# A cross-attention and FFN layer on one core: new instruction sequences on all engines, with some sums and small steps moved

## The reference

```python
sim = (ctx @ Wq.T per head) . (ctx @ Wk.T per head), summed over 4 heads, scaled      # 512 x 512 per batch
threshold = the 153rd largest of each row of sim
A = sigmoid(sim) * (sim >= threshold);  A = (A + A.T) * 0.5
g = sigmoid(gamma_raw)
x = x + (1 - g) * layernorm(x) + g * A
z = layernorm(x)
# bitlinear(v, w): v is RMS-normed and rounded to 8 bits per row, w is rounded to -1, 0, 1 by its mean |w|
x = x + bitlinear(silu(bitlinear(z, w_gate)) * bitlinear(z, w_up), w_down)
```

## Time and profile before

| what | us |
|---|---|
| median of 3 runs (lowest, highest) | 289.45 (288.89, 290.41) |
| the profiled execution's own time | 291.13 |
| its span, first to last instruction | 289.3 |
| first gate matmul to the last final | 75.3 to 286.9 |
| busy: TensorE, VectorE, ScalarE, GpSimd | 212.6, 226.1, 191.9, 191.7 |

### The profile page before, as it was taken

The page is one execution under the profiler, slowest core; times in us unless marked ns, Lnnn a source line. Parts: engine busy times, 40 slices in busy tenths (PEclk is TensorE's granted clock), DMA queues, the critical chain, the costliest instruction groups (busy, mean ns, idle before and its releaser), DMA issues.

```text
span 289.3 us, 3730 instructions
## 1 busy us (share of the span) xinstructions
PE 212.6 (73%) x916; PEld 99.6 (34%) x926; DVE 226.1 (78%) x355; ACT 191.9 (66%) x352; POOL 191.7 (66%) x380
## 2 busy tenths in 40 slices
PE   7760001322888876979995997798979999999874
PEld 6320001320333333434342543333344444444332
DVE  0388784998979999899859889989879994959621
ACT  2697799899979979976475899732427643731500
POOL 2156778877897966788878867787754774507330
PEclk9996555575599999999998899999979999999999
DMA  5999999937840794331321643205030534180592
GB/s 134 381 387 365 365 210 377 278 134 219 162 95 19 121 184 82 74 68 36 61 71 22 178 76 72 56 0 128 3 72 0 106 96 91 27 192 13 110 243 109
DMA packets 78970, 39.21 MB, mean 136 GB/s; under 512 B 67936, under 2 KB 70240, under 8 KB 78432
## 3 DMA queue, kind: packets, MB, share of 16 engines
q1 hardware_dynamic: 78944, 38.94, 53.7%
HBM read 17.96 MB, written 4.19 MB: 77 GB/s over the span
## 4 chain that ended last, share of the span: by engine, by line
PE 24%; POOLq 23%; issue 17%; POOL 17%; ACT 8%; DVE 7%; DVEq 2%; ACTq 0%
PE DN L380 8%; PE U L366 8%; PE G L352 7%; POOLq L809 4%; POOLq L839 3%; POOL S L899 3%; POOLq L811 3%; POOL X L835 2%; POOL X L842 2%; ACT S L513 2%; POOLq L799 2%; ACT WuT L506 2%; ACT junk_c L464 2%; POOL srch L812 2%; POOL sig L783 2%
## 5 line engine op out<-in xcount | busy, mean ns | idle before, releaser
L489 ACT ACTIVATE sg<-G,gsc 128x1024 f32<-128x1024 f32 x32 | 35.5, 1110 | 48.7 <-PE G L352 38.3
L366 PE MATMUL U<-WuT,xqT 128*128 128x512 bf16 x256 | 63.5, 393 | 5.3 <-DVE S L670 5.3
L352 PE MATMUL G<-WgT,xqT 128*128 128x512 bf16 x256 | 62.2, 387 | 3.8 <-ACT sg L489 3.8
L380 PE MATMUL DN<-WdT,S 128*128 128x512 bf16 x246 | 56.7, 380 | 8.7 <-DVE X L696 8.2
L670 DVE TENSOR_TENSOR S<-U,sg 128x1024 f32<-128x1024 f32 x32 | 39.0, 1219 | 12.8 <-PE U L366 9.0
L899 POOL TENSOR_SCALAR S<-S,qh 128x2048 int16<-128x2048 f32 x16 | 31.8, 1990 | 25.6 <-DVE qh L686 24.9
L464 ACT ACTIVATE junk_c<-rows,srch 128x512 int8<-128x512 f32 x64 | 45.3, 711 | 5.1 <-POOL srch L812 4.3
L380 PEld LDWEIGHTS DN<-WdT,S 128*128 128x128 bf16 x256 | 24.8, 98 | 40.8 <-issue 12.9
L366 PEld LDWEIGHTS U<-WuT,xqT 128*128 128x128 bf16 x256 | 25.1, 101 | 39.2 <-DVE S L670 9.9
L352 PEld LDWEIGHTS G<-WgT,xqT 128*128 128x128 bf16 x256 | 25.1, 100 | 36.6 <-issue 5.5
L675 DVE TENSOR_REDUCE amh<-S 128x1 f32<-128x2048 f32 x16 | 36.4, 2274 | 0.1
(11 more groups left out here) (127 smaller groups left out, 382.3 us busy)
## 6 DMA issues: line engine op xcount, KB each, us to landing
S<-in_L_ffn_w_gate SPq DMA_DIRECT2D x4, 1024.0 KB, 10.3
X<-in_x SPq DMA_DIRECT2D x4, 1024.0 KB, 7.0
S<-in_L_ffn_w_up SPq DMA_DIRECT2D x4, 1024.0 KB, 13.8
S<-in_L_ffn_w_down SPq DMA_DIRECT2D x4, 1024.0 KB, 9.3
out<-X SPq DMA_DIRECT2D x16, 256.0 KB, 2.6
C<-in_ctx SPq DMA_DIRECT2D x2, 256.0 KB, 5.8
C<-in_ctx SPq DMA_DIRECT2D x1, 512.0 KB, 13.9
xqT<-qx SPq DMA_TRANSPOSE x16, 2.5
```

The source lines that it names most:

```text
L352: last = nc.tensor.matmul(G[:, c * 512:(c + 1) * 512], xqT[:, t, k, :], WgT[:, 4 * n:4 * n + 4, k, :], start=(k == 0), stop=(k == KD - 1))
L366: last = nc.tensor.matmul(U[:, c * 512:(c + 1) * 512], xqT[:, t, k, :], WuT[:, 4 * n:4 * n + 4, k, :], start=(k == 0), stop=(k == KD - 1))
L380: last = nc.tensor.matmul(DN[:, :], hqT[:, i % 2, k, :], WdT[:, k, :], start=(k == 0), stop=(k == KF - 1))
L489: A(sg[:, u % 2, :], G[:, :], ACT.Silu, scale=gsc[:, b % 2, t:t + 1]).then_inc(silu_done, 1)
```

## The change

All five lists are in another order. Beside that: the sums of the search (mean and variance of half a row of sim) come from VectorE's `bn_stats` and `bn_aggr` (`sim_stats`) and no longer from ScalarE, and the first threshold is three GpSimd instructions instead of eight; all four sums of w_down are on ScalarE (three were on VectorE); `x_scale`, `x_round` and `x_cast` of the first batch go tile by tile; the reciprocal of hfl moved from GpSimd (a power of -1) to VectorE (`h_floor`); `ln_coef` has fewer steps; for the last tile the absolute maximum, the rounding (now on VectorE), the cast and the transpose go by halves; and the last four downs write four different banks, so that they no longer wait for each other's `final`.

```diff
+        def down_bank(i):
+
+            return (DN, AT, SIM, TR)[i % NT] if i >= TILES - NT else DN
 
...
-        ABS_ACT = ((1,), (0, 1, 2, 3), (3,))
+        ABS_ACT = ((1,), (0, 1, 2, 3), (0, 1, 2, 3))
...
+            def hT_last(hs):
+                i = TILES - 1
+                sp.wait_ge(hq_last, hs + 1)
+                sp.wait_ge(down_psum, i - 1)
+                sp.dma_start_transpose(hqT[:, i % 2, hs * KF // 2:(hs + 1) * KF // 2, :],
+                                       hq[:, i % 2, hs * HF:(hs + 1) * HF]).then_inc(hqT_last[hs], 16)
+
...
-            w_load(0, w_gate, 0); w_load(0, w_gate, 1); c_load(0, 1, 2); x_load(0); w_load(0, w_gate, 2)
...
+            x_load(0); c_load(0, 1, 2); w_load(0, w_gate, 0); w_load(0, w_gate, 1); w_load(0, w_gate, 2)
+            w_load(0, w_gate, 3); w_load(1, w_up, 0); c_load(1, 2, 4); x_load(1); w_load(1, w_up, 1); x_load(2)
+            w_load(1, w_up, 2); w_load(1, w_up, 3); w_load(2, w_down, 0); w_load(2, w_down, 1); w_transpose(0, 0)
...
+                if i == TILES - 1:
+                    pe.wait_ge(hqT_last[hs], 16)
+                elif hs == 0:
+                    pe.wait_ge(hqT_ready[i % 2], 16 * (i // 2 + 1))
                 if hs == 0:
-                    pe.wait_ge(hqT_ready[i % 2], 16 * (i // 2 + 1))
...
+                    elif i <= TILES - NT:
+                        pe.wait_ge(final_done, i)
                     else:
-                        pe.wait_ge(final_done, i)
+                        pe.wait_ge(x1_ready, NT * B)
                 for k in range(hs * KF // 2, (hs + 1) * KF // 2):
-                    last = nc.tensor.matmul(DN[:, :], hqT[:, i % 2, k, :], WdT[:, k, :],
+                    last = nc.tensor.matmul(down_bank(i)[:, :], hqT[:, i % 2, k, :], WdT[:, k, :],
...
-                    if a:
-                        act.wait_ge(thr_act, 2 * ROUNDS * (a - 1) + j // 2 + 1)
-                    A(ROWS[a % 2][:, j, :], sim_bank(a, j), ACT.Copy, accum_out=sum1[:, j:j + 1]).then_inc(sim_ready, 1)
-
-            def sim_sq(a, j):
-
-                act.wait_ge(sim_ready, NT * a + j + 1)
-                if NT * a + j >= 2:
-                    act.wait_ge(simstat, NT * a + j - 1)
-                A(junk_s[:, j % 2, :], ROWS[a % 2][:, j, 0:N // 2], ACT.Square, accum_out=sum2[:, j:j + 1]).then_inc(simstat, 1)
+                    A(ROWS[a % 2][:, j, :], sim_bank(a, j), ACT.Copy).then_inc(sim_ready, 1)
...
+            def sim_stats(a, *js):
+
+                for j in js:
+                    dve.wait_ge(sim_ready, NT * a + j + 1)
+                    V.bn_stats(bns[:, j, :], ROWS[a % 2][:, j, 0:N // 2])
+                dve.drain()
+                for j in js:
+                    last = V.bn_aggr(mvs[:, j, :], bns[:, j, :])
+                last.then_inc(simstat, 1)
 
...
+            def x_scale(a, *js):
+
+                c = slice(js[0], js[-1] + 1)
+                dve.drain()
+                V.tensor_scalar(amf[:, c], amx[:, c], D * Q_EPS * (LN_EPS * RMS_EPS) ** 0.5, 1.0 / 127.0,
+                                ALU.max, ALU.mult)
+                dve.drain()
+                V.reciprocal(qsx[:, c], amf[:, c]).then_inc(qsx_ready, len(js))
...
+            def last_absmax(hs):
+
+                i = TILES - 1
+                dve.wait_ge(mul_done, 2 * i + hs + 1)
+                V.tensor_reduce(amh[:, i % 4:i % 4 + 1] if hs == 0 else aml[:, 0:1],
+                                h[:, i % 2, hs * HF:(hs + 1) * HF], AX.X, ALU.max, apply_absolute_value=True)
+
+            def last_scale():
+                i, c = TILES - 1, slice((TILES - 1) % 4, (TILES - 1) % 4 + 1)
+                dve.wait_ge(hcoef, i - 3)
+                dve.drain()
+                V.scalar_tensor_tensor(amh[:, c], amh[:, c], aml[:, 0:1], hfl[:, (B - 1) % 2, NT - 1:NT],
+                                       ALU.max, ALU.max)
+                dve.drain()
+                V.tensor_scalar(amc[:, c], amh[:, c], 1.0 / 127.0, None, ALU.mult)
+                dve.drain()
+                V.reciprocal(qh[:, c], amc[:, c]).then_inc(qh_ready, 1)
+
+            def last_round(hs):
+                i, f = TILES - 1, slice(hs * HF, (hs + 1) * HF)
+                dve.drain()
+                if hs == 0:
+                    dve.wait_ge(hqT_ready[i % 2], 16 * (i // 2))
+                V.tensor_scalar(hq[:, i % 2, f].bitcast(I16), h[:, i % 2, f], qh[:, i % 4:i % 4 + 1], 1.0,
+                                ALU.mult, ALU.mult)
+                dve.drain()
+                V.tensor_copy(hq[:, i % 2, f], hq[:, i % 2, f].bitcast(I16)).then_inc(hq_last, 1)
+
+            def h_floor(a):
+
+                dve.wait_ge(xcoef, a + 1)
+                V.reciprocal(hfl[:, a % 2, :], hfl[:, a % 2, :])
+
...
-                pool.wait_ge(simstat, NT * a + 2 * p + 2)
-                G_.tensor_scalar(sims_m[:, js], sum1[:, js], 1.0 / N, 0.0, ALU.mult, ALU.add)
-                G_.tensor_scalar(sd[:, js], sum2[:, js], 2.0 / N, 0.0, ALU.mult, ALU.add)
-                pool.drain()
-                G_.tensor_tensor(ptmp[:, js], sims_m[:, js], sims_m[:, js], ALU.mult)
-                pool.drain()
-                G_.tensor_tensor(sd[:, js], sd[:, js], ptmp[:, js], ALU.subtract)
-                pool.drain()
-                G_.tensor_scalar(sd[:, js], sd[:, js], 0.0, 1.0, ALU.max, ALU.mult)
-                pool.drain()
-                G_.tensor_tensor(sd[:, js], sd[:, js], bc(root, 2), ALU.pow)
+                pool.wait_ge(simstat, 2 * a + p + 1)
+                G_.tensor_tensor(sd[:, js], mvs[:, js, 1], bc(root, 2), ALU.pow)
                 pool.drain()
                 G_.tensor_scalar(ptmp[:, js], sd[:, js], -START_Z, 0.0, ALU.mult, ALU.add)
                 pool.drain()
-                G_.tensor_tensor(nthr[:, js], ptmp[:, js], sims_m[:, js], ALU.subtract).then_inc(thr_act, 1)
+                G_.tensor_tensor(nthr[:, js], ptmp[:, js], mvs[:, js, 0], ALU.subtract).then_inc(thr_act, 1)
 
...
-                G_.tensor_tensor(su2[:, a % 2, :], usc[:, a % 2, :], usc[:, a % 2, :], ALU.mult)
-                pool.drain()
-                G_.tensor_tensor(hfl[:, a % 2, :], hfl[:, a % 2, :], bc(inv, NT), ALU.pow).then_inc(xcoef, 1)
-
```

243 lines of the change are left out of this document (121 added, 122 removed).

## The result

The changed kernel takes 285.15 us in the median (284.09 to 286.1, 4 runs), the kernel before beside it 289.17 (288.72 to 290.41): a ratio of 0.985, 95% interval 0.9811 to 0.9888. The profiled execution took 285.98 us with a span of 284.2, against 291.13 and 289.3. The prediction was 288.4, so the kernel became faster, and by more than forecast: 4.0 us between the medians and 5.1 us between the profiled spans, where the sum said 1.05.

The account below looks back on a forecast made before the run. VectorE was taken to set T, the last batch's first transpose, with fixed TensorE work and the tail behind it. From 289.45: -2.3 + 3.45 + 3.45 - 5.65 = -1.05 gave 288.4 us; range 283.5 to 294, forecast's own 286 to 290.8.

Parts of the forecast that it names:

- Start (-0.5): Head up to about 91 us: new load order and moved sums put VectorE 0.5 us ahead.
- Rival 3: Start of the FFN late: first gate at 76.5, second at 88; 291.4 us if 3 us get through; chance 0.07.
- T: Moment of TensorE's first transpose of A of the last batch, 211.37 us before; forecast to move -2.3, to about 209.
- VectorE's added work up to T (+4.0): VectorE before the last batch's transposes: search sums, reciprocals and `mul(19)` added, `final(6)` removed; +4.0 us.
- The waits (-3.3): VectorE's waits from 91.5 to 211.3 us, 5.3 us without the branch, shrink by 3.3 us.
- The stretching (-2.5): VectorE's mask products and quantizations running longer than needed, 5.0 us in all; half goes, -2.5 us.
- Rival 1: VectorE hung on GpSimd; all its waits and stretching go, T moves -6.8, time 283.9 us; chance 0.22.
- The sign of being wrong in kind: TensorE reaching the last batch's transposes after the mask was ready would mean TensorE bounds the middle; no size given.
- Rival 2: Slower: added sums fall on VectorE, the full engine, and nothing comes back; T +3.5, time 294.2 us; chance 0.20.
- Rival 4: Collisions of VectorE with GpSimd stay, waits shrink: the stretching's 2.5 us don't come, 290.9 us; chance 0.08.
- Behind T (+6.9): TensorE after the last batch's first transpose: `down(7)` and `down(12)` now run there, +3.45 us each.
- Tail (-5.65): From the last up's end to the program's end: 15.1 us in place of 20.75, -5.65 us.

Follow-up runs that it names:

- run 3: Changed kernel with the last batch's four mask products one behind the other after `mul(19)`; 0.993 of the kernel before.
- run 2: Changed kernel with five small GpSimd instructions added ahead of each first threshold, search sums still on VectorE; 1.010 of the kernel before.
- Run 9: Kernel before with only the search sums moved to VectorE and the first threshold cut to three GpSimd instructions; 1.019 of the kernel before.
- Run 4: Changed kernel with three of w_down's four sums back on VectorE; 0.999 of the kernel before.
- run 12: Changed kernel with four list moves against waits, then `mul(16)` and others moved earlier too; 0.987 of the kernel before.
- Runs 5 and 6: Changed kernel with one bank for all downs, 0.995 of the kernel before; changed kernel with the last tile whole again, 1.000.
- Runs 1: Changed kernel with the search sums back on ScalarE and the first threshold again in eight GpSimd instructions; 1.017 of the kernel before.

## Why the prediction was right or wrong

*Start (-0.5).* First weight sum at 12.87 (said 12.4), first gate at 76.46 (76.5), second gate at 90.83 (said 88). But VectorE is not ahead at 91 us. A row of before, then one of after:

```profile
90.36 1.22 DVE L670 TENSOR_TENSOR S<-U,sg 128x1024 f32<-128x1024 f32 x1
```

```profile
92.03 1.21 DVE L688 TENSOR_TENSOR S<-U,sg 128x1024 f32<-128x1024 f32 x1
```

The first is `mul(1)`, the second `mul(0)`. So at 91.0 the changed kernel lacks two `mul`, 2.4 us, that the kernel before had done at 91.5, and is one mask product (0.7) ahead: +1.2 and not -0.5. Rival 3's lateness was there; by T it was more than made good.

*VectorE's added work up to T (+4.0).* Sized about right. By count and mean of the lines the sums added 3.5 us (a pair 0.75 + 0.25 as said, 414 ns for a `bn_stats` of 256 elements), the floors 0.5 and `mul(19)` 1.2, and 0.5 of `final(6)` went behind T: +4.7. With the two `mul` and the mask product of the start it is 6.4 us more in the stretch. Against it stands an item that the prediction didn't have: where one VectorE instruction follows another without a pause, their rows overlap by some 0.08 us, and the durations less the busy time are 1.6 us more after than before.

*The waits (-3.3).* The size came out, in part by luck. VectorE's time without an instruction is 119.8 - 106.03 = 13.8 us before and 116.0 - 105.82 = 10.2 after, -3.6. The waits alone (eight groups before, not seven) fell by as much, 9.2 to 5.6; the short pauses stayed. Of the 5.3 us that I had bounded 3.6 are left, -1.7 and not -3.3. The other 2.0 are the gap between two `pick` products, which I had taken for the branch's and left out. It lay beside GpSimd's products, so it probably belongs to the same collisions as the stretching; that is argued from the rows, and no run moved it alone.

*The stretching (-2.5).* This is the term that was most off. It gave -4.9: the mask products -3.6 (all of my bound), the quantizations -1.0, `rank`'s product +1.7, and the small products over eight elements 8 x (430 - 224) = -1.6, with 0.4 in smaller ones; I had seen none of these last as stretched. I took half where all came, since I tied the stretching to GpSimd's big tiles, which stay. What counts is which instruction stands beside them: run 3 shows that the order of four calls is worth 753 against 997 ns.

In all: the stretch begins 0.5 earlier, and 6.4 of work, -4.9 of stretching, -1.6 of overlap and -3.6 of waits give -4.2, where T moved by -4.4; the rest is rounding. Against the forecast's -2.3 the start was 1.7 us worse and the work 0.7, the stretching 2.4 better, the waits 0.3 better, and the overlap, 1.6, was not in the sum.

*Rival 1 (GpSimd was what VectorE hung on).* Its price of -6.8 at T was not reached, but run 2 speaks for its mechanism: forty small GpSimd instructions cost 7 us of the total, and in the head they stand ahead of a sum that VectorE waits for. Run 9 limits it: in the old lists the relief, together with the sums on VectorE, gives nothing.

*The sign of being wrong in kind.* I had written that TensorE reaching the transposes after the mask was ready would mean that TensorE bounds the middle. It did, by 0.15 us. Run 4 says that the reading would be false: VectorE work added in the head, while ScalarE had less, moved T by 4.4 us, and again no wait is seen there. TensorE's own arrival hangs on VectorE's products ahead of it, here `mul(16)`, and in run 12, where that comes early, TensorE waits for VectorE at three later places. The sign was badly chosen.

*Rival 2 (added sums on the full engine).* It did not come in the new lists, and it is what run 9 shows in the old ones: 1.019. The points that the prediction gives for it are wrong by its own sum: with -0.5 + 4.0 at T, 6.9 behind and -5.65 in the tail the time moves by 4.75 less what VectorE saves, so the zero lies at 4.75 us of the 10.3 and not at 1.0, and a loss that can be told (1.45 us) at 3.3 and not at 2.5. The forecast of 5.8 saved was 1.05 from no change at all.

*Rival 4 and the rule on SBUF.* The Trainium skill (SBUF — State Buffer, "Who interferes with whom") says that a VectorE instruction with two SBUF inputs contends with a GpSimd instruction that reads SBUF. For an instruction with one input the same section of the Trainium skill rules this out only outside the 2-port modes, which `cast` and `tensor_scalar` can enter, and the prediction left that exception out. This case agrees on the first: the mask products, `rank`'s product and the `pick` products have two inputs, while the reductions of 2048 columns stayed at 2277 ns. The stretched ones with a single input are of the kinds of the exception: the quantizations (1159 and 810 ns in the mean, where the median of all eight is 690), and in run 12 a cast and one of the two instructions on four columns; the other has two inputs. GpSimd's big instructions ran beside all three of run 12 (rows above). No run shows whether these were in such a mode. And I drew the wrong thing from the rule, that the collisions would stay because the big instructions do.

*Behind T (+6.9).* Measured +5.2. The two downs are 3.45 each, but I took what stood behind T as fixed, and 1.7 us of it were TensorE's slow clock after its wait before: the up at 212.51 had taken 3.37 us at a granted clock of 0.56, with the stretch's clock at 0.97, now 1.89 and 1.00. In this execution the wait cost twice, and I counted it once. It doesn't always: in run 9 the same wait of 2.23 us was followed by a clock of 1.00 and an up of 1.90 us.

The row on TensorE right behind T (start, duration, what), before and then in run 9:

```profile
212.51 3.37 PE L366 MATMUL U<-WuT,xqT 128*128 128x512 bf16 x8
```

```profile
217.85 1.90 PE L364 MATMUL U<-WuT,xqT 128*128 128x512 bf16 x8
```

*Tail (-5.65).* Right within 0.3 us: -5.9, with its parts, `down(15)` 8.2 us behind the last up and 15.0 to the end. Runs 5 and 6 were expected to cost 2.8 and 3.5 us. Their spans are 3.0 and 3.5 longer, but that they fit is luck, since T came 1.8 and 1.6 us earlier in these executions; the tails themselves are 4.8 and 5.1 longer. Most of the missing part is the down that ran slow behind its wait, 1.4 and 1.7 us, which neither expectation had; the ratios, 1.0 and 1.5%, are 2.8 and 4.2 us. Moving `down(12)` was worth nothing that can be told, as expected.

*The sum.* -1.05, then -2.1 at T, -1.7 behind it and -0.2 in the tail: -5.1 between the profiled executions, and 4.0 between the medians. The time of 285.15 lay in the range and in the lower part, outside the forecast's own range of 286 to 290.8.

What stays open: which part of the new lists pays for the sums' move. Runs 1 and 9 bound it from both sides, no run separates it. Also not tested apart: fewer steps in `ln_coef`, the floors on VectorE, the scales of the first batch tile by tile, and the new order of the loads.
